# Two attention stages re-staged: queries and keys split in two, stacked to 48 rows a head through DRAM, and one unrolled pipeline over 128 heads

## The chip, the cores and the metric

The kernel runs on one core of one Trainium2 chip. The metric is the device time of one execution in microseconds (us). The kernel before took 2926.12 us, the median of three runs (2922.68 to 2927.64).

## The reference

Four transformer layers work one after the other on 8 sequences of 256 tokens, 256 channels, in float32. Each layer is an attention and a feed-forward part, each adding to x. Layers 0 and 3 have the same kind of attention, and only that is touched here:

```python
xn = layernorm(x)                       # (8, 256, 256)
q = xn @ Wq.T + bq;  k = xn @ Wk.T + bk;  v = xn @ Wv.T + bv
# 16 heads of 16 channels
scores = q_h @ k_h.T * 0.25             # causal, (256, 256) for each of 8 x 16 heads
x += concat(softmax(scores) @ v_h) @ Wo.T + bo
```

The other stages (two mixtures of experts before and after, the mixed attention of layer 1, the linear attention of layer 2, the dense feed-forward parts) stay as they are.

## The kernel before

Both stages are calls of `attention_small`, `a0` for layer 0 and `a3` for layer 3. The engines run their own instruction lists and meet at semaphores. The input xT lies in SBUF transposed: channels on partitions, tokens along the row. A batch is one of the 8 sequences. A loop (`Fori`) runs over seven batches and the eighth follows it; the 16 heads of a batch are written out.

For each batch, TensorE (`project`) multiplies the batch's 256 tokens, which GpSimd copied into `xb`, by the weights of keys, queries and values, into four PSUM tiles `ring0` to `ring3`. The bias of the values, and later that of the output, is one more matmul with a single row. A head has only 16 channels. So that a plain 128-row contraction gives the scores of one head, the keys are written 16 times into `kT`, each time multiplied by a column of `heads` that is 1 on that head's 16 channels and 0 elsewhere: ScalarE writes heads 0 to 7 (L1337) and VectorE heads 8 to 15 (L1376). Queries are used whole.

A head then passes through this chain. TensorE makes the scores, causal, in two matmuls (L1267: 128 queries by 128 keys; L1268: 128 by 256). VectorE scales and masks them from PSUM to `s` (L1388) and takes the negated maximum of each of the two row blocks (L1392). ScalarE takes the exponential and its row sums (L1349, with its accumulator reads). VectorE inverts the sums (L1398). GpSimd multiplies by the inverse (L1222), and after every second head sends one indirect DMA (L211) which carries token rows to the mixture of experts. TensorE turns the result in three transposes (`turn`, L1276). ScalarE copies even heads (L1359) and VectorE odd heads (L1404) to `pT`. TensorE multiplies by the values (`values`, L1288 and L1290) into `pv`; the value tile `v` is spaced so that each head's output lands on its own 16 partitions.

Within a batch the scores run four heads ahead of the turning (`AHEAD`). At a batch's end they do not run ahead: TensorE finishes the 16 heads, projects the next batch, waits for the copies, makes the first four scores, and then the output projection of the batch that ended (L1320, bias L1322), which VectorE adds to x (L1419).

SP issues the weight loads at a stage's start, in `a0` followed by the 10 MB of expert weights for the next stage (L1213, tile `wres`, 128 partitions of 16 x 1216 floats). No other plain DMA runs in these stages.

Of the kernel before, what the change touches and what calls it, by code (L numbers as in the profile page):

```python
# [9 lines left out]
ALU = mybir.AluOpType  # L10
# [7 lines left out]
P = 128  # L18
# [1117 lines left out]
AHEAD = 4  # L1136
SUMS_AHEAD = 3
SLOTS = 2 * AHEAD
# [3 lines left out]
def attention_small(nc, name, const, xT, w, scale, send, resident=()):  # L1142

    with ExitStack() as ctx:
        sp = Space(nc, ctx, name)  # L1150
        wts = {n: sp.sb(n, [P, KD, D]) for n in ("wq", "wk", "wv", "wo")}
        bq = sp.sb("bq", [P, KD])
        bk = sp.sb("bk", [P, KD])
        bv = sp.sb("bv", [1, D])
        bo = sp.sb("bo", [1, D])
        heads = sp.sb("heads", [P, HC])
        bkh = sp.sb("bkh", [P, HS])
        xb = sp.sb("xb", [P, KD, SEQ])
        qT = sp.sb("qT", [P, KD, SEQ])
        kT = sp.sb("kT", [P, HS, SEQ])  # L1160
        v = sp.sb("v", [P, QT * KD, HC * VS])
        s = sp.sb("s", [P, SLOTS, SC])
        nmax = sp.sb("nmax", [P, SLOTS, QT])
        rsum = sp.sb("rsum", [P, HS, QT])
        rinv = sp.sb("rinv", [P, HS, QT])
        pT = [sp.sb(f"pT{i}", [P, SC]) for i in range(2)]
        oT = sp.sb("oT", [P, KD, SEQ])
        ring = [sp.ps(f"ring{i}", [P, 512]) for i in range(4)]
        pv = sp.ps("pv", [P, KD, SEQ])
        ppT = [sp.ps(f"ppT{i}", [P, 512]) for i in range(2)]  # L1170
        pend = sp.ps("pend", [P, 512])
        w_in = sp.sem("w_in")
        bkh_ready = sp.sem("bkh_ready")
        xb_ready = sp.sem("xb_ready")
        q_done = sp.sem("q_done")
        k_done = sp.sem("k_done")
        v_done = sp.sem("v_done")
        q_ready = sp.sem("q_ready")
        k0_ready = sp.sem("k0_ready")
        k1_ready = sp.sem("k1_ready")  # L1180
# [4 lines left out]
        exp_ready = sp.sem("exp_ready")  # L1185
        turned = sp.sem("turned")
# [3 lines left out]
        inv_ready = sp.sem("inv_ready")  # L1190
        o_ready = sp.sem("o_ready")
        scaled = sp.sem("scaled")
        v_zeroed = sp.sem("v_zeroed")
        out_done = sp.sem("out_done")
        added = sp.sem("added")
        ident, ones, cmask = const["ident"], const["ones"], const["cmask"]
        spans = ((0, P), (P, SC))

        def batches(eng, run):

            with eng.Fori(0, NB - 1) as b:
                run(b, True)
            run(NB - 1, False)

        with nc.Block() as block:
            @block.sync
            def _(sync):
                for n in ("wq", "wk", "wv", "wo"):
                    sync.dma_start(wts[n][:, :, :], w[n]).then_inc(w_in, 16)
                for to, n in ((bq, "bq"), (bk, "bk"), (bv, "bv"), (bo, "bo"), (heads, "heads")):  # L1210
                    sync.dma_start(to[:, :], w[n]).then_inc(w_in, 16)
                for to, of, loaded in resident:
                    sync.dma_start(to, of).then_inc(loaded, 16)  # L1213

            @block.gpsimd
            def _(pool):
                def scale_rows(b, h):

                    pool.wait_ge(inv_ready, b * HS + (h + 1))
                    for t, (lo, hi) in enumerate(spans):  # L1220
                        rows = s[:, h % SLOTS, lo:hi]
                        last = nc.gpsimd.tensor_tensor(rows, rows, rinv[:, h, t:t + 1].broadcast_to([P, hi - lo]),  # L1222
                                                       ALU.mult)
                    last.then_inc(scaled, 1)

                def run(b, more):
                    for h in range(HS):
                        scale_rows(b, h)
                        if h % 2:
                            send(b * (HS // 2) + h // 2)  # L1230
                        if more and h == HC:

                            pool.wait_ge(v_done, b + 1)
                            nc.gpsimd.tensor_copy(xb[:, :, :], xT[:, :, bass.ds(b * SEQ + SEQ, SEQ)]
                                                  ).then_inc(xb_ready, 1)

                nc.gpsimd.tensor_copy(xb[:, :, :], xT[:, :, 0:SEQ]).then_inc(xb_ready, 1)
                for b in range(NB):
                    run(b, b + 1 < NB)

            @block.tensor
            def _(pe):
                def project(b):

                    pe.wait_ge(xb_ready, b + 1)
                    for n, bank, done in (("wk", 1, k_done), ("wq", 0, q_done)):
                        for c in range(KD):
                            to = ring[bank + c] if n == "wk" else ring[bank]
                            at = 0 if n == "wk" else c * SEQ
                            for k in range(KD):  # L1250
                                last = nc.tensor.matmul(to[:, at:at + SEQ], wts[n][:, k, c * P:(c + 1) * P], xb[:, k, :],  # L1251
                                                        start=(k == 0), stop=(k == KD - 1))
                        last.then_inc(done, 1)
                    for t in range(QT):
                        for k in range(KD):
                            nc.tensor.matmul(ring[3][:, t * D:(t + 1) * D], xb[:, k, t * P:(t + 1) * P],
                                             wts["wv"][:, k, :], start=(k == 0), stop=False)
# [1081 lines left out]
```

## Time and profile before

| | |
|---|---|
| median of 3 runs | 2926.12 us |
| the profiled execution | 2925.24 us |
| its span, first to last instruction | 2923.5 us |
| mean granted TensorE clock | 0.894 |
| busy, share of the span: PE, DVE, ACT, POOL | 79%, 54%, 45%, 32% |
| stage a0, by the timeline | 94.5 to 432.8 us |
| stage a3, by the timeline | 2393.6 to 2734.9 us |

The shares are averages over some twenty stages with different limits; the two stages at issue make up 680 of the 2924 us. PE is TensorE's matmul, PEld its weight load, DVE VectorE, ACT ScalarE, POOL GpSimd, SPq the queue that issues DMAs. A float32 matmul appears as two records.

### The profile page before, as it was taken

The page shows a single profiled execution, that of the slowest core. Times are in us where ns is not written, and L with a number is a line of the kernel's source. Part 1 is how long each engine was busy: PE and PEld are TensorE (multiplying, and loading weights), DVE is VectorE, ACT ScalarE, POOL GpSimd, SP SyncE. Part 2 cuts the span into 40 slices and gives each one's busy share as a digit, 9 for nine tenths or more (in the row PEclk, how much of TensorE's full clock was granted, in tenths as well). Part 3 has the DMA queues.
Part 4 walks back from the last instruction along what each step waited for, and adds up shares of the span by engine and source line. Part 5 has one row for each costly group of instructions (what it writes and reads, how often), then busy time and mean ns, then how long its engine had stood idle before and what let it go on. Part 6 is the DMA issues. An engine that isn't in the chain of part 4 may idle for free. (4 is left out here: it accounts for less than half of the span.)

```text
span 2923.5 us, 40558 instructions
## 1 busy us (share of the span) xinstructions
PE 2296.0 (79%) x11552; PEld 1807.6 (62%) x11552; DVE 1591.0 (54%) x4140; ACT 1322.2 (45%) x4166; POOL 927.1 (32%) x1053
## 2 busy tenths in 40 slices
PE   3599989997469999999998973468991229999787
PEld 2477776665247777777787762456880217777666
DVE  3677762224346666776684235553334577766324
ACT  1355553331157666666674121464770105555321
POOL 0355550005233333333340000540007006555325
PEclk9999999997689999999999985788995559999788
DMA  5400012323300000000000100611543000000354
GB/s 211 164 25 25 25 38 89 93 89 116 123 0 1 1 1 1 1 1 1 1 1 28 48 25 2 252 54 45 161 147 103 16 15 23 5 1 1 122 164 140
DMA packets 95446, 172.41 MB, mean 59 GB/s; under 512 B 17875, under 2 KB 73135, under 8 KB 93625
## 3 DMA queue, kind: packets, MB, share of 16 engines
q1 hardware_dynamic: 76856, 126.47, 12.7%
q0 software_dynamic: 18432, 44.05, 4.8%
q8 instruction: 74, 1.21, 0.2%
q14 instruction: 84, 0.68, 0.1%
HBM read 111.76 MB, written 65.01 MB: 60 GB/s over the span
## 5 line engine op out<-in xcount | busy, mean ns | idle before, releaser
L1222 POOL TENSOR_TENSOR a_s<-a_s,a_rinv 128x128 f32<-128x128 f32 (+1 forms) x512 | 243.3, 505 | 263.5 <-DVE a_rinv L1398 259.5
L1349 ACT ACTIVATE a_s<-a_s,a_nmax 128x128 f32<-128x128 f32 (+1 forms) x512 | 227.7, 446 | 181.5 <-DVE a_nmax L1392 177.2
L851 POOL DMA_INDIRECT f_yg<-y,l_slot x128 | 126.3, 987 | 383.8 <-issue 366.6
L1789 POOL TENSOR_TENSOR a_rcos<-a_qk,a_cos 128x1280 f32<-128x1280 f32 x32 | 93.2, 2911 | 403.8 <-ACT a_qk L1963 403.8
L211 POOL DMA_INDIRECT xg<-all_xn,l_slot_d x192 | 194.0, 1011 | 39.3 <-issue 39.3
L605 DVE TENSOR_TENSOR e_hid<-e_gate,e_pG 128x128 f32<-128x128 f32 (+1 forms) x192 | 59.3, 309 | 234.5 <-ACT e_gate L580 234.5
L1288 PE MATMUL a_pv<-a_pT,a_v 128*128 128x256 f32 x512 | 161.1, 397 | 17.8 <-ACT a_pT L1359 17.8
L2063 DVE SCALAR_TENSOR_TENSOR a_s<-a_pS,all_cmask 128x384 f32<-128x384 f32 x128 | 71.4, 558 | 172.9 <-PE a_pS L1870 172.9
L1268 PE MATMUL a_ring<-a_kT,a_qT 128*128 128x256 f32 x512 | 163.4, 403 | 0.0
L1392 DVE TENSOR_REDUCE a_nmax<-a_s 128x1 f32<-128x128 f32 (+1 forms) x512 | 156.7, 348 | 8.8
L1388 DVE SCALAR_TENSOR_TENSOR a_s<-a_ring,all_cmask 128x384 f32<-128x384 f32 x256 | 139.9, 547 | 25.0 <-PE a_ring L1268 22.5
L183 PE MATMUL n_pT<-all_ident,all_xn 128*128 128x128 f32 x128 | 33.9, 411 | 145.8 <-DVE all_xn L173 141.9
L494 POOL DMA_INDIRECT e_yg<-y,l_slot x64 | 61.0, 953 | 266.7 <-SPq L468 246.9
L1337 ACT ACTIVATE a_kT<-a_ring,a_bkh,a_heads 128x256 f32<-128x256 f32 x128 | 60.1, 575 | 181.7 <-PE a_ring L1251 181.7
L890 ACT ACTIVATE f_gate<-f_pg 128x512 f32<-128x512 f32 x60 | 35.9, 599 | 223.9 <-PE f_pg L770 223.9
L1276 PE MATMUL a_ppT<-all_ident,a_s 128*128 128x128 f32 x768 | 128.0, 276 | 8.0 <-POOL a_s L1222 8.0
L1896 PE MATMUL a_pout<-a_wo,a_oT 128*128 128x256 f32 x512 | 131.9, 380 | 2.4 <-ACT a_oT L2002 1.4
L1831 PE MATMUL a_pq<-a_wq,all_xT 128*128 128x512 f32 x256 | 123.8, 607 | 9.8 <-ACT a_qk L1963 9.8
L952 DVE TENSOR_TENSOR f_hid<-f_gate,f_pu 128x512 f32<-128x512 f32 x60 | 41.3, 688 | 157.0 <-PE f_pu L770 119.2
L1972 ACT ACTIVATE a_e<-a_qk,a_top 128x128 f32<-128x128 f32 x320 | 123.5, 390 | 1.5 <-DVE a_top L2039 1.5
L1799 POOL TENSOR_TENSOR a_src<-a_rcos,a_rsin 128x1280 f32<-128x1280 f32 x32 | 94.2, 2944 | 84.7 <-PE a_pt L1859 84.4
L528 PE MATMUL e_pG<-l_wres,e_xgT 128*128 (+1 forms) x448 | 119.0, 388 | 1.8 <-ACT e_xgT L573 1.8
(289 smaller groups left out, 6481.5 us busy)
## 6 DMA issues: line engine op xcount, KB each, us to landing
e_xs<-xg SPq DMA_DIRECT2D x176, 128.0 KB, 2.2
y<-e_ys SPq DMA_DIRECT2D x176, 128.0 KB, 1.7
l_wres<-in_L_resident SPq DMA_DIRECT2D x3, 4224.0 KB
xg<-blank_zeros SPq DMA_DIRECT2D x4, 3072.0 KB
s_w<-in_L_bank SPq DMA_DIRECT2D x32, 384.0 KB, 4.0
l0e_wres<-in_L_resident SPq DMA_DIRECT2D x4, 2432.0 KB
f_w<-in_L_bank SPq DMA_DIRECT2D x16, 448.0 KB, 3.2
f_w<-in_L_shared SPq DMA_DIRECT2D x14, 448.0 KB, 3.7
```

The lines of the kernel that those rows point to most:

```text
L211: nc.gpsimd.indirect_dma_start(out=xg[:, :], out_offset=bass.IndirectOffsetOnAxis(ap=slot_d[:, t, j:j + 1], axis=0), in_=xn[:, t, :], in_o ...
L851: nc.gpsimd.indirect_dma_start(out=yg[i % GR][:, :], out_offset=None, in_=y, in_offset=bass.IndirectOffsetOnAxis(ap=slot[:, t, j:j + 1], a ...
L1222: last = nc.gpsimd.tensor_tensor(rows, rows, rinv[:, h, t:t + 1].broadcast_to([P, hi - lo]), ALU.mult)
L1268: nc.tensor.matmul(ring[h % 4][:, P:SC], qT[:, c, P:SEQ], kT[:, h, :], start=True, stop=True).then_inc(s_done, 1)
L1276: last = nc.tensor.transpose(ppT[h % 2][:, i * P:(i + 1) * P], s[:, h % SLOTS, i * P:(i + 1) * P], ident[:, :])
L1288: nc.tensor.matmul(pv[:, c, :], v[:, c, j * P:(j + 1) * P], pT[h % 2][:, 0:SEQ], start=first, stop=final, skip_group_check=True)
L1349: last = nc.scalar.activation(s[:, h % SLOTS, lo:hi], s[:, h % SLOTS, lo:hi], ACT.Exp, bias=nmax[:, h % SLOTS, t:t + 1], accum_out=rsum[:, ...
L1388: nc.vector.scalar_tensor_tensor(out=s[:, h % SLOTS, :], in0=ring[h % 4][:, 0:SC], scalar=scale, in1=cmask[:, :], op0=ALU.mult, op1=ALU.ad ...
L1392: last = nc.vector.tensor_reduce(nmax[:, h % SLOTS, t:t + 1], s[:, h % SLOTS, lo:hi], AX_X, ALU.max, negate=True)
L1831: last = nc.tensor.matmul(pq[:, :], tokens(b, k, t), wq[:, k, gr, :], start=(k == 0), stop=(k == KD - 1))
L1896: last = nc.tensor.matmul(pout[:, t, :], oT[H % 2][:, t * P:(t + 1) * P], wo[:, n % HKV * GQ + h, :], start=(h == 0 and t == 0), stop=(h = ...
L1972: last = nc.scalar.activation(e[:, t, h, :], qk[:, t, h, :], ACT.Exp, bias=top[:, at:at + 1], accum_out=total[:, at:at + 1])
```

## The change

`attention_small` is rewritten. The parts:

- **Projection in pieces.** Queries and keys are projected in pieces of 128 output channels by 512 tokens (two batches, a chunk): four pieces a chunk, 16 a stage, into one PSUM tile `pj`. ScalarE writes the biased piece rounded to fp32r (`hi`), VectorE the rest (`lo` = exact minus `hi`).
- **Through DRAM.** SP stores both parts to `qk_rows`, and loads them back stacked: for each head 48 rows, queries (hi, lo, hi), keys (hi, hi, lo), so that one fp32r contraction over 48 rows gives hi*hi + lo*hi + hi*lo. Even heads lie at partitions 0 to 47, odd ones at 64 to 111. A load of half a batch (8 heads) is 12 DMAs of 64 KB, 64 runs of 1 KB each; 24 a batch, and four stores of 256 KB a batch.
- **Scores** are two fp32r matmuls from those tiles, in a ring of two PSUM tiles in place of four.
- **One list of slots.** The batch loop goes; 128 heads a stage run in one unrolled sequence. In slot n, TensorE makes scores n+4, turns n and applies values n-1; ScalarE takes exponentials n+3 and then rounds the slot's piece (`round_piece`); VectorE inverts n+2, masks and takes maxima n+4, and then makes `lo` (`rest_piece`). Slots run from -24 to 131. The pieces of a chunk are put 24 slots ahead, every third slot; a batch's values are projected in two halves, 6 slots ahead; its output two slots after its last head.
- **Biases.** The bias of the values is added by VectorE as it copies them; that of the output is added to x once, by GpSimd, at the stage's start. The single-row matmuls, `xb` and its copies, `heads`, `bkh` and the 16 masked key copies go.
- **Copies.** `pv` and `oT` are double, and `oT` is copied by ScalarE. The expert weights of `a0` are issued behind the first two loads, not at once.

```diff
-        kT = sp.sb("kT", [P, HS, SEQ])
+        stack = [[sp.sb(f"{n}s{i}", [P, HC // 2, SEQ], F32R) for i in range(2)] for n in "qk"]
-        ring = [sp.ps(f"ring{i}", [P, 512]) for i in range(4)]
+        ring = [sp.ps(f"ring{i}", [P, 512]) for i in range(2)]
...
+        def piece_at(slot):
+            c, left = divmod(slot + LEAD, 2 * HS)
+            return 4 * c + left // 3 if left % 3 == 0 and left < 12 and 0 <= c < NC else None
...
+                def store(i):
+                    c, n, k = PIECES[i]
+                    for part, ready, tiles, out in ((0, hi_ready, hi, hi_out), (1, lo_ready, lo, lo_out)):
+                        sync.wait_ge(ready, i + 1)
+                        sync.dma_start(qk_rows[n, part, k * P:(k + 1) * P, c * CHUNK:(c + 1) * CHUNK],
+                                       tiles[i % 2][:, :].bitcast(F32)).then_inc(out[i % 2], 16)
+                def load(b, half):
+                    c = b // 2
+                    for i in range(2):
+                        sync.wait_ge(hi_out[i], 16 * 2 * (c + 1))
+                        sync.wait_ge(lo_out[i], 16 * 2 * (c + 1))
+                    after(sync, s_done, HS * b + HC * (half - 1))
+                    for n, parts in ((0, (0, 1, 0)), (1, (0, 0, 1))):
+                        for odd in range(2):
+                            for j, part in enumerate(parts):
...
+                                sync.dma_start(stack[n][half][at:at + DH, :, :].bitcast(F32), rows).then_inc(stacked[half], 16)
+                for i in range(4):
+                    store(i)
+                for c in range(NC):
+                    load(2 * c, 0)
+                    load(2 * c, 1)
+                    if c == 0:
+                        for to, of, loaded in resident:
+                            sync.dma_start(to, of).then_inc(loaded, 16)
+                    load(2 * c + 1, 0)
+                    if c + 1 < NC:
+                        for i in range(4 * c + 4, 4 * c + 8):
+                            store(i)
+                    load(2 * c + 1, 1)
...
+                def piece(i):
+                    c, n, k_out = PIECES[i]
+                    after(pe, hi_ready, i)
+                    after(pe, lo_ready, i)
...
+                    for k in range(KD):
+                        last = nc.tensor.matmul(pj[:, :], wts[("wq", "wk")[n]][:, k, k_out * P:(k_out + 1) * P],
+                                                xT[:, k, c * CHUNK:(c + 1) * CHUNK], start=(k == 0), stop=(k == KD - 1))
+                    last.then_inc(piece_done, 1)
...
+                def scores(H):
+                    b, h = divmod(H, HS)
+                    half, a, r = h // HC, h % HC // 2, 64 * (h % 2)
+                    if h % HC == 0:
+                        pe.wait_ge(stacked[half], 16 * 12 * (b + 1))
+                    after(pe, s_read, H - 1)
+                    q, k = (stack[n][half][r:r + ST, a, :] for n in range(2))
+                    nc.tensor.matmul(ring[H % 2][:, 0:P], q[:, 0:P], k[:, 0:P], start=True, stop=True)
+                    nc.tensor.matmul(ring[H % 2][:, P:SC], q[:, P:SEQ], k[:, :], start=True, stop=True).then_inc(s_done, 1)
...
+                for slot in SLOTS_ALL:
+                    if 0 <= slot + 4 < NH:
+                        scores(slot + 4)
+                    i = piece_at(slot)
+                    if i is not None:
+                        piece(i)
+                    if 0 <= slot < NH:
+                        turn(slot)
...
+                    if 0 <= slot - 1 < NH:
+                        values(slot - 1)
...
+                def round_piece(i):
+                    n, k = PIECES[i][1:]
+                    act.wait_ge(piece_done, i + 1)
+                    after(act, hi_out[i % 2], 16 * (i // 2))
+                    after(act, lo_ready, i - 1)
+                    nc.scalar.activation(hi[i % 2][:, :], pj[:, :], ACT.Identity,
+                                         bias=bias[n][:, k:k + 1]).then_inc(hi_ready, 1)
...
+                def rest_piece(i):
+                    dve.wait_ge(hi_ready, i + 1)
+                    after(dve, lo_out[i % 2], 16 * (i // 2))
+                    nc.vector.scalar_tensor_tensor(out=lo[i % 2][:, :], in0=pj[:, :], scalar=bias[n][:, k:k + 1],
+                                                   in1=hi[i % 2][:, :], op0=ALU.add, op1=ALU.subtract).then_inc(lo_ready, 1)
```

## Rows read from the trace of the kernel before

**Rows 1.** Windows: length, busy us of PE, PEld, DVE, ACT, POOL, then granted clock, DMA share, GB/s

```profile
95.00:114.00 19.00, 9.85 (x28) 7.03 (x28) 8.66 (x12) 4.49 (x10) 0.17 (x1) 1.00 0.96 373
194.00:234.00 40.00, 37.78 (x218) 31.06 (x217) 28.84 (x84) 23.07 (x84) 23.79 (x41) 1.00 0.07 26
2480.00:2520.00 40.00, 39.02 (x216) 32.42 (x216) 28.63 (x82) 21.94 (x79) 22.84 (x40) 0.96 0.02 6
1800.00:1950.00 150.00, 74.40 (x343) 62.25 (x344) 89.22 (x169) 69.63 (x142) 69.21 (x72) 0.76 0.38 149
```

**Rows 2.** Timeline of PE, one head in mid-batch (start, length, idle before)

```profile
167.10 0.39 PE L1267 MATMUL a_ring<-a_kT,a_qT 128*128 128x128 f32 x2
167.32 0.60 PE L1268 MATMUL a_ring<-a_kT,a_qT 128*128 128x256 f32 x2
167.75 0.49 PE L1276 MATMUL a_ppT<-all_ident,a_s 128*128 128x128 f32 x3
168.08 0.60 PE L1288 MATMUL a_pv<-a_pT,a_v 128*128 128x256 f32 x2
...
168.74 0.39 PE L1267 MATMUL a_ring<-a_kT,a_qT 128*128 128x128 f32 x2
```

**Rows 3.** Timeline of PE between two batches

```profile
188.43 1.89 PE L1251 MATMUL a_ring<-a_xb,a_wk 128*128 128x256 f32 x8
...
191.89 1.03 PE L1256 MATMUL a_ring<-a_wv,a_xb 128*128 128x256 f32 x4
...
196.10 0.46 PE L1267 MATMUL a_ring<-a_kT,a_qT 128*128 128x128 f32 x2 [0.88 <-DVE a_v L1380]
...
198.79 1.03 PE L1320 MATMUL a_pend<-a_wo,a_oT 128*128 128x256 f32 x4
...
202.06 0.49 PE L1267 MATMUL a_ring<-a_kT,a_qT 128*128 128x128 f32 x2
```

**Rows 4.** Timeline of POOL: first and last work of both stages, one boundary

```profile
119.78 1.89 POOL L1222 TENSOR_TENSOR a_s<-a_s,a_rinv 128x128 f32<-128x128 f32 x4 [24.61 <-DVE a_rinv L1398]
...
201.80 1.89 POOL L1222 TENSOR_TENSOR a_s<-a_s,a_rinv 128x128 f32<-128x128 f32 x4 [14.53 <-DVE a_rinv L1398]
...
204.90 1.89 POOL L1222 TENSOR_TENSOR a_s<-a_s,a_rinv 128x128 f32<-128x128 f32 x4
...
424.98 1.01 POOL L211 DMA_INDIRECT xg<-all_xn,l_slot_d  x1 [0.16 <-issue]
...
2414.98 1.89 POOL L1222 TENSOR_TENSOR a_s<-a_s,a_rinv 128x128 f32<-128x128 f32 x4 [20.72 <-DVE a_rinv L1398]
...
2727.10 1.01 POOL L211 DMA_INDIRECT xg<-all_xn,l_slot_d  x1 [0.16 <-issue]
```

**Rows 5.** Timeline of DVE, start and end of two heads' work

```profile
171.56 0.56 DVE L1404 COPY a_pT<-a_ppT 128x384 f32<-128x384 f32 x1 [0.37 <-PE a_ppT L1276]
...
174.32 0.15 DVE L1398 RECIPROCAL a_rinv<-a_rsum 128x2 f32<-128x2 f32 x1
```

**Rows 6.** One line's instructions: duration ns min/median/max, first and last start

```profile
L907 DVE TENSOR_TENSOR f_wl<-f_w,f_wh x30: 683/684/726, 676.1 to 2896.7; 128x512 fp32r<-128x512 f32 x30
```

**Rows 7.** Timeline of PE, the first projections of both stages

```profile
103.35 3.78 PE L1251 MATMUL a_ring<-a_xb,a_wk 128*128 128x256 f32 x8 [26.25 <-DMA a_heads<-in_heads]
...
2399.95 3.55 PE L1251 MATMUL a_ring<-a_xb,a_wk 128*128 128x256 f32 x8 [39.98 <-DMA a_heads<-in_heads]
```

**Rows 8.** Timeline of PE, fp32r matmuls of another stage

```profile
684.25 0.39 PE L770 MATMUL f_pu<-f_xh,f_wl 128*128 128x512 f32 x1
684.48 0.39 PE L770 MATMUL f_pu<-f_xh,f_wh 128*128 128x512 f32 x1
```

**Rows 9.** Timeline of SPq, an issue behind big transfers and one in an idle queue

```profile
35.40 1.25 SPq L271 DMA_DIRECT2D r_order<-in_order  x1
...
95.39 0.42 SPq L1209 DMA_DIRECT2D a_wv<-in_L_wv  x1
```

**Rows 10.** DMA issues: KB each, median us from issue to landing

```profile
e_xs<-xg SPq DMA_DIRECT2D x176, 128.0 KB, 2.2
y<-e_ys SPq DMA_DIRECT2D x176, 128.0 KB, 1.7
```

More of the change, by code:

```diff
@@ L1151, in attention_small @@
         wts = {n: sp.sb(n, [P, KD, D]) for n in ("wq", "wk", "wv", "wo")}
[L1152 to L1159, printed above, removed]
-        kT = sp.sb("kT", [P, HS, SEQ])
+        bias = [sp.sb(f"bias{i}", [P, KD]) for i in range(2)]
+        bvb = sp.sb("bvb", [P, D])
@@ L1189, in attention_small, with after, batch_at @@
         pv_done = sp.sem("pv_done")
-        inv_ready = sp.sem("inv_ready")
         o_ready = sp.sem("o_ready")
-        scaled = sp.sem("scaled")
-        v_zeroed = sp.sem("v_zeroed")
         out_done = sp.sem("out_done")
         added = sp.sem("added")
[L1196 to L1203, printed above, removed]
+        ident = const["ident"]
+        spans = ((0, 0, P), (1, P, SC))
+        PIECES = [(c, n, k) for c in range(NC) for n in range(2) for k in range(KD)]
+        def after(eng, sem, value):
+            if value > 0:
+                eng.wait_ge(sem, value)
+        def piece_at(slot):
+            c, left = divmod(slot + LEAD, 2 * HS)
+            return 4 * c + left // 3 if left % 3 == 0 and left < 12 and 0 <= c < NC else None
+        def batch_at(slot, ahead):
+            b, left = divmod(slot + ahead, HS)
+            return b if left == 0 and 0 <= b < NB else None
+        SLOTS_ALL = range(-LEAD, NH + 4)
         with nc.Block() as block:
@@ L1223, in scale_rows @@
+                for H in range(NH):
+                    pool.wait_ge(inv_ready, H + 1)
+                    for t, lo_, hi_ in spans:
+                        rows = s[:, H % RING, lo_:hi_]
+                        last = nc.gpsimd.tensor_tensor(rows, rows, rinv[:, H % RING, t:t + 1].broadcast_to([P, hi_ - lo_]),
                                                        ALU.mult)
                     last.then_inc(scaled, 1)
[L1226 to L1235, printed above, removed]
@@ L1237, in _ @@
-                nc.gpsimd.tensor_copy(xb[:, :, :], xT[:, :, 0:SEQ]).then_inc(xb_ready, 1)
-                for b in range(NB):
-                    run(b, b + 1 < NB)
+                    if H % 2:
+                        send(H // 2)
             @block.tensor
             def _(pe):
[L1243 to L1253, printed above, removed]
+                sent = {"pieces": 0, "values": 0}
```

318 lines of the change are left out of this document (148 added, 170 removed).

## The prediction

> **What bounds the kernel now.** The table of windows comes first. In both stages PE is busy 38 to 39 of every 40 us, DVE 29, ACT 23, POOL 24 [rows 1]. A busy PE may be waiting in the array, so the next view is PE's timeline in mid-batch: one head takes 1.64 us (167.10 to 168.74) without a gap, of which scores 0.65, turning 0.33, values 0.65 or 0.66 [rows 2]. POOL's timeline shows the same from the other side: two heads in 3.10 us back to back (201.80 to 204.90), that is 1.55 a head, and then 14.53 us of nothing at the boundary of two batches [rows 4]. PE's timeline there says what fills the hole: projection from 188.43 to the wait that ends at 196.10, four heads' scores until 198.79, output projection until 202.06 [rows 3]. So the stage is PE, head by head, plus a boundary at which the pipe empties. A batch takes 39.87 us in a0 by the starts of POOL's bursts. POOL works from 119.78 to 426.0 in a0 (306.2 us) and from 2414.98 to 2728.1 in a3 (313.1 us) [rows 4].
>
> **PE's work for a batch after the change.** Turning 16 x 0.33 = 5.3 and values 16 x 0.65 = 10.4 stay [rows 2]. The pieces cost what the projection of q and k costs now: 188.43 to 191.89, 3.46 us a batch, since the product is the same size [rows 3]. Values are four 256-column float32 matmuls' worth, half of 3.46, 1.73; output the same 1.73, in place of 198.79 to 202.06 = 3.27, because the bias matmuls go [rows 3]. Scores: no row has an fp32r matmul as narrow as 128 or 256 columns or with 48 rows. The nearest are fp32r with 512 columns, started every 0.23 us [rows 8], against four times that for float32 (a 256-column one takes 0.43 [rows 2]). In proportion 384 columns would take 0.17. The weight loads set a floor: the transposes, 128 columns each, follow each other at 0.11 [rows 2], and two score matmuls have two weight loads, 0.22. The upper end is no gain at all, 0.65. I take 0.22, nearest the fp32r rows, so 3.5 a batch. Sum 5.3 + 10.4 + 3.5 + 3.5 + 1.7 + 1.7 = 26.1 us (33.0 at the upper end).
>
> **DVE.** Two heads occupy it from 171.56 to 174.47, 2.91 us, so 23.3 for 16 [rows 5]. It loses eight masked key copies and the copy of oT. It gains two `lo` pieces of 512 elements (0.68 each by the row of the same form [rows 6], 0.72 with the step to the next), two value copies of 256 elements, which I put at 0.42 each (between 0.29 and 0.68 in proportion), and keeps the add to x at about 0.7. Sum 23.3 + 1.4 + 0.8 + 0.7 = 26.3. **POOL**: 8 x 3.10 = 24.8 [rows 4]; the copy of xb goes, the bias add of 4096 elements lies at the start, under the prologue below. **ACT**: 23.0 now [rows 1], less ten key and query copies of 0.46 (4.6), plus two `hi` pieces and one oT copy of about 0.6: 20.3.
>
> So PE 26.1, DVE 26.3 and POOL 24.8 stand side by side, and the pace is a little over the largest, because they wait for each other. The place is a piece slot. There PE has scores 0.22, a piece 1.73, turning and values, 2.9 us; ScalarE can round only after the piece, and VectorE, in order, stands at `lo` behind it: piece 1.73 + 0.6 + semaphores = 2.4 us after the scores, while its own masking and maxima take 1.1. Some 1.2 us are lost unless PE is ahead of DVE, and two score tiles let it be ahead by about one head. Three slots with one piece cost DVE 3 x 1.46 + 0.7 + 0.3 left over = 5.4; 12 of 32 slots are of that kind: 21.6 us. The other 20 go at POOL's 1.55 or DVE's 29.1 + 3.2 of values and adds, plus waits for the value projections: 34. That is 55.6 for two batches, **28 us a batch**. From below it is 26.3 (DVE alone). 8 x 28 = 224 in place of 306.2 and 313.1: **-171 us**.
>
> **The prologue.** Now it is from the end of the weight wait (103.35, 2399.95) to POOL's first work, 16.4 and 15.0 us [rows 4, 7]. After: four pieces in series, since `pj` is one tile. PE ran its first eight records of 256 columns in 3.5 to 3.8 us [rows 7] where it takes 1.73 later [rows 3]: it had stood idle for 26 and 40 us, and runs at the lower of its two levels (1.2 and 2.4 GHz) at first. A piece is the same work: 3.4 cold or 1.7 warm, then hi 0.6, lo 0.7, semaphores 0.2. One or two cold, the rest warm: 16.5 (13 to 20). Then the last stores, issue 0.9 and landing near 2 (128 KB out took 1.7 [rows 10]): 3. Then 12 loads issued at 0.47 (0.42 and the step [rows 9]), 5.6, and landing 2.2 [rows 10]: 7.8. Then the chain of the first head, 5.7 as now. Together 33, so +16.6 in a0, less 2 because the expert weights no longer compete with the weights (the window before carries 373 GB/s [rows 1]), and +18 in a3: **+33**. The drain loses two bias matmuls on its path: **-2**.
>
> **The new wait: SP's order.** A chunk's first three quarters are loaded well ahead. But load (2c+1, second half) is queued behind the four stores of the next chunk. Their last piece is in slot 32c+17, and the load is needed by scores 32c+24 in slot 32c+20. From `lo` ready: two stores 0.9, 12 loads 5.6, landing 2.2, 8.7 us; cover is the rest of slot 17 and slots 18 and 19, 3.8. PE then stands in scores with turning and values behind it, POOL runs dry two heads later. About 5 us, three times a stage: **+30** for both. If stores and loads land as they issue it is 3 each, if they queue 7. In a0 the first load of batch 1 is also behind the expert weights: 10 MB at 373 GB/s [rows 1] is 26.7 us, started about 3.4 after the first scores; needed about 26 after them. Landing near 33: **+7** (0 if the queue interleaves).
>
> **Sum**: 2925.2 - 171 + 33 - 2 + 30 + 7 = 2822 us. The profiled execution, 2925.24, is 0.9 below the median, which is nothing here. About 0.2% (6 us) is what a measurement can tell from no change.
>
> **A rule weighed.** PE's clock was granted in full in a0 and 0.96 in a3 with PE 95% busy or more, 0.76 in a stretch where it was busy half the time [rows 1]. The new pipe has PE at 26.1 of 28, with more and shorter waits. The Trainium skill (TensorE: Matmul & The Clock Gate, Part 1) says that the array runs at half rate by default, that activity releases it and idleness brings it back. By that rule the prologue, with PE idle for some 11 us between pieces and scores, starts the pipe at 1.2 GHz; the rows of both first projections agree. The same page (Why this matters for your kernels, the row on small-K matmuls) says that a 32-row matmul takes as long as a 128-row one and gains only where row groups run together; then the 48 rows themselves save nothing and the gain is the single fp32r pass. By the first rule with every piece of both prologues at 1.2 GHz, an estimate, the time would be 2832; by the rows, which let one or two pieces be slow, it is 2822, and the sum goes by these.
>
> **Rivals.**
> - *Little is lost between the engines.* For it: PE leads by one head, and POOL has slack in piece slots. Pace 26.5, the SP waits at 3: 2822 - 24 - 12 = 2786, and 2760 with no SP waits. Against: three engines within 6%, each in order, rarely meet their own sum. Chance 0.22, times 2760 to 2795.
> - *PE is dearer.* Narrow fp32r matmuls gain less, or the clock slips. If the 128-column one stays at its present 0.22 and the other at 0.11, PE is 27.9, pace 29.5: +24, 2846 (still within my forecast). With no gain in scores PE is 33, pace 34: 2918. With a mean clock of 0.87: 30 + 1.5 = 31.5 a batch, 2878. Chance 0.20 for 2860 to 2918.
> - *The clock stays low and the kernel is slower.* This decides at the pace that eats the gain: 28 + 103/16 = 34.4 us a batch. PE's 26.1/c + 1.5 reaches it at a granted clock of 0.79. At the 0.76 of the window of another stage [rows 1] it is 35.8: +125, 2947. For it: shorter bursts, a PE that waits in piece slots. Against: what PE has to do fills 93% of the pace even at 2.4 GHz, and a slower clock makes it busier. Chance 0.05.
> - *SP's issue bounds.* 28 DMAs a batch at 0.47 are 13 us. In a busy queue one issue took 1.25 [rows 9]; then they are 35 us a batch, and the prologues grow by 19: 2822 + 112 - 30 + 19 = 2923, no change. Against: 2 MB a batch is 75 GB/s, a fifth of what the window of 373 GB/s carried. Chance 0.03, half of it on the slow side.
>
> **Numbers.** Forecast 0.50, times 2795 to 2860. Faster by over 0.2%: 0.50 + 0.22 + 0.20 + half of what stays, 0.92; within 0.2%: 0.02; slower 0.06. The range takes the forecast, two thirds of the low rival and half of the dear one: 2770 to 2885.
>
> **What would show it.** Masked key copies and single-row matmuls gone; PE's scores near 0.22 a head; POOL's idle at batch boundaries gone and its pace 1.7 to 1.8 a head; first POOL work 33 us after the weights; three waits of PE on stacked loads of some 5 us a stage, in slots 32c+20, and one of some 7 early in a0; ACT about 20 us a batch. Wrong if PE's clock falls under 0.9, if DVE waits for `hi` over 1 us at each piece, or if loads take over 1 us to issue.

## The result and the profile after

| | before | after |
|---|---|---|
| median | 2924.40 us (4 runs) | 2889.32 us (4 runs, 2883.79 to 2896.41) |
| ratio | | 0.9886 (95%: 0.9854 to 0.9918) |
| span of the profiled execution, clock | 2923.5 us, 0.894 | 2881.9 us, 0.882 |
| stage a0, first a_wq issue to first load of the next stage | 339.1 us | 325.3 us |
| stage a3 | 343.4 us | 319.4 us |

The change makes the kernel 1.1% faster. The forecast was 2822 us with a range from 2770 to 2885, so the time lies 4 us above the range and 67 above the forecast.

POOL's timeline, first and last work of both stages, answers to [rows 4]:

```profile
131.19 0.97 POOL L1267 TENSOR_TENSOR a_s<-a_s,a_rinv 128x128 f32<-128x128 f32 x2 [20.65 <-DVE a_rinv L1430]
...
412.57 1.01 POOL L211 DMA_INDIRECT xg<-all_xn,l_slot_d  x1 [0.16 <-issue]
...
2419.15 0.97 POOL L1267 TENSOR_TENSOR a_s<-a_s,a_rinv 128x128 f32<-128x128 f32 x2 [22.52 <-DVE a_rinv L1430]
...
2692.04 1.01 POOL L211 DMA_INDIRECT xg<-all_xn,l_slot_d  x1 [0.16 <-issue]
```

From first to last work, called the pipe below, it is 282.4 us in a0 (306.2 before) and 273.9 in a3 (313.1). The prologues, from a stage's start to that first work, grew by 11.4 us in a0 (131.19 against 119.78) and by 16.7 in a3 (38.1 against 21.4). Over both stages the pipes give -63, the prologues +28 and the ends -3, together -38 of the 41.6 us by which the spans differ.

PE's timeline, one plain head in mid-batch, answers to [rows 2]:

```profile
281.44 0.60 PE L1325 MATMUL a_pv<-a_pT,a_v 128*128 128x256 f32 x2
281.87 0.38 PE L1327 MATMUL a_pv<-a_pT,a_v 128*128 128x128 f32 x2
282.19 0.32 PE L1306 MATMUL a_ring<-a_ks,a_qs 48*128 48x128 f32 x1
282.35 0.33 PE L1307 MATMUL a_ring<-a_ks,a_qs 48*128 48x256 f32 x1
282.61 0.55 PE L1313 MATMUL a_ppT<-all_ident,a_s 128*128 128x128 f32 x3
283.00 0.60 PE L1325 MATMUL a_pv<-a_pT,a_v 128*128 128x256 f32 x2
```

The starts tell what each part costs. Scores, 282.19 to 282.61, are 0.42 us (0.65 before, 0.22 forecast). But turning became 0.39 (0.33), and from the second values matmul to the next scores it is 0.32 where it was 0.22. A head is 1.56 us, not the forecast's 1.20, and was 1.64. PE has no gap in it. The weight loads at the same place:

```profile
281.87 0.19 PEld L1327 LDWEIGHTS a_pv<-a_pT,a_v 128*128 128x128 f32 x1
282.18 0.18 PEld L1306 LDWEIGHTS a_ring<-a_ks,a_qs 48*128 48x128 f32 x1
...
282.61 0.31 PEld L1313 LDWEIGHTS a_ppT<-all_ident,a_s 128*128 128x128 f32 x3
```

The load for the scores starts at 282.18 and its matmul at 282.19; that of the turning at 282.61 together with its matmul. On both edges of the 48-row pair nothing is loaded ahead of its matmul by more than 0.01 us.

PE's timeline at its waits for stacked loads, with SP's below:

```profile
127.86 0.48 PE L1306 MATMUL a_ring<-a_ks,a_qs 48*128 48x128 f32 x2 [8.60 <-DMA a_ks<-qk_rows]
...
164.72 0.47 PE L1306 MATMUL a_ring<-a_ks,a_qs 48*128 48x128 f32 x1 [5.59 <-DMA a_ks<-qk_rows]
...
191.56 0.47 PE L1306 MATMUL a_ring<-a_ks,a_qs 48*128 48x128 f32 x1 [3.67 <-DMA a_ks<-qk_rows]
...
265.10 0.47 PE L1306 MATMUL a_ring<-a_ks,a_qs 48*128 48x128 f32 x1 [4.35 <-DMA a_ks<-qk_rows]
```

```profile
254.79 0.32 SPq L1227 DMA_DIRECT2D qk_rows<-a_hi  x1
255.57 0.39 SPq L1227 DMA_DIRECT2D qk_rows<-a_lo  x1
256.13 4.38 SPq L1242 DMA_DIRECT2D a_qs<-qk_rows  x6
260.55 2.78 SPq L1242 DMA_DIRECT2D a_ks<-qk_rows  x6
```

The last store leaves at 255.57, the twelve loads behind it are issued until 263.3, and PE resumes at 265.10. The first of the four waits is the prologue's. A fifth wait in a0 is 2.84; a3 has 2.94, 4.19 and 3.98 beside its prologue. Without the prologues that is 16.5 and 11.1 us. What a wait leaves behind is in the windows (columns as in [rows 1]):

```profile
160.00:164.00 4.00, 0.00 (x0) 0.00 (x0) 0.19 (x2) 0.00 (x0) 0.96 (x2) 1.00 1.08 337
164.00:168.00 4.00, 3.28 (x11) 2.65 (x11) 1.24 (x4) 1.40 (x5) 0.97 (x2) 0.52 0.25 95
168.00:172.00 4.00, 4.00 (x12) 2.76 (x12) 2.44 (x7) 0.98 (x4) 1.97 (x3) 0.50 0.09 33
172.00:176.00 4.00, 4.00 (x13) 2.10 (x11) 0.97 (x3) 1.26 (x4) 0.00 (x0) 0.70 0.00 0
...
204.00:208.00 4.00, 4.00 (x27) 3.40 (x28) 3.40 (x12) 3.06 (x12) 3.05 (x6) 1.00 0.09 33
...
226.00:262.00 36.00, 34.58 (x177) 25.25 (x175) 26.62 (x79) 21.49 (x77) 23.46 (x40) 1.00 0.34 116
262.00:297.00 35.00, 31.90 (x176) 26.22 (x177) 24.40 (x76) 19.50 (x74) 23.59 (x40) 0.90 0.32 92
```

PE stood idle from 159.1 to 164.7. Then the granted clock is 0.50, its lower level of 1.2 GHz, for some 9 us, although PE is busy 4.00 of 4 us: 12 or 13 records in a window where 27 run at the full clock. Behind the other waits it is 5 to 10 us in a0 and 5 to 13 in a3, some 63 us behind all seven. The first heads of each pipe also run at 0.50, in a0 from 127.9 to 140. The clock over both pipes is 0.92 and 0.93.

The new pieces of work in a0 (groups by line, mean ns after the comma):

```profile
L1406 DVE SCALAR_TENSOR_TENSOR a_lo<-a_pj,a_bias,a_hi 128x512 fp32r<-128x512 f32 x16 | 12.0, 751 | 34.0 <-ACT a_hi L1367 34.0
L1367 ACT ACTIVATE a_hi<-a_pj,a_bias 128x512 fp32r<-128x512 f32 x16 | 11.0, 689 | 74.2 <-PE a_pj L1284 74.2
L1413 DVE TENSOR_TENSOR a_v<-a_pj,a_bvb 128x256 f32<-128x256 f32 x16 | 6.8, 423 | 3.5 <-PE a_pj L1295 2.6
```

In the order of these lines, the forecast had 680, 600 and 420 ns.

### The profile page after: what moved, and what is told of

The parts are those of the page before. It is cut to its first block and busy times, and to the rows that moved or that the text cites. A ratio compares the mean times of both kernels' runs of the same rounds, so it can differ in the third digit from the quotient of the medians.

```text
span 2881.9 us, 38632 instructions
## 1 busy us (share of the span) xinstructions
PE 2228.6 (77%) x10912; PEld 1715.8 (60%) x10912; DVE 1539.7 (53%) x4040; ACT 1285.0 (45%) x4054; POOL 942.1 (33%) x1039
## 5 line engine op out<-in xcount | busy, mean ns | idle before, releaser
L1313 PE MATMUL a_ppT<-all_ident,a_s 128*128 128x128 f32 x768 | 148.6, 306 | 0.0
L1306 PE MATMUL a_ring<-a_ks,a_qs 48*128 48x128 f32 x256 | 87.5, 345 | 47.9 <-DMA a_ks<-qk_rows 45.1
L2105 DVE SCALAR_TENSOR_TENSOR a_s<-a_s,a_rinv,a_g 128x128 f32<-128x128 f32 (+1 forms) x256 | 117.4, 500 | 4.5
```

Source lines behind the costliest of these rows:

```text
L1313: last = nc.tensor.transpose(ppT[H % 2][:, i * P:(i + 1) * P], s[:, H % RING, i * P:(i + 1) * P], ident[:, :])
```

## The experiments

Four theories are tested: *rows* (scores on 48 rows keep weights from being loaded ahead, so a head costs 0.35 us more), *clock* (PE pays for each wait a second time at half clock), *queue order* (a wait comes from what stands ahead of the loads on SP), and the rival *GpSimd or VectorE sets the pace*. Kernels that ran once are compared by the spans of their profiled executions: 2881.9 us is that of the changed kernel. The spans of its four runs go from 2881.9 to 2894.5, so a few us between two kernels mean nothing. Diffs are against the changed kernel unless said; lines left out are marked by three dots.

| kernel | median (runs) | span | clock |
|---|---|---|---|
| earlier pieces | 2857.21 (4), ratio 0.9773 (0.9750 to 0.9797) | 2861.5 | 0.886 |
| float32 scores | 3066.68 (1) | 3064.8 | 0.856 |
| scores twice | 3000.46 (1) | 2998.6 | 0.862 |
| half of GpSimd's work | 2881.40 (1) | 2879.5 | 0.883 |
| 128 rows | 2837.61 (4), ratio 0.970 (0.966 to 0.974) | 2837.9 | 0.882 |
| 128 rows, twice | 2852.59 (1) | 2850.8 | 0.879 |
| 128 rows, float32 | 2888.52 (1) | 2886.7 | 0.889 |
| earlier pieces, experts' weights later | 2864.61 (4), ratio 0.980 (0.976 to 0.984) | 2862.9 | 0.886 |
| the three together | 2827.21 (6), ratio 0.9663 (0.9632 to 0.9694) | 2827.4 | 0.886 |
| 128 rows, earlier pieces, weights spread | 2804.17 (5), ratio 0.9587 (0.9569 to 0.9605) | 2803.8 | 0.891 |
| the same with filler | 2806.71 (5), ratio 0.9600 (0.9581 to 0.9619) | 2803.8 | 0.893 |
| the same (no filler), half of GpSimd's work | 2803.31 (1) | 2801.5 | 0.890 |

**Earlier pieces.** The pieces of a chunk start 30 slots ahead.

```diff
-    LEAD = 24
+    LEAD = 30
```

> The four pieces of the next chunk are put 30 slots ahead in place of 24, so that their stores leave SP's queue before slot 32c+12 and the last quarter's loads are issued in time. Theory W (SP's order makes PE wait, and each wait is followed by a stretch at the lower clock): the three later waits of PE on the stacked loads in each stage go (some 11 us in a0, 11 in a3), and the windows of 35 us with a granted clock of 0.86 to 0.90 go to 1.00, worth another 10 to 13 us a stage; the span falls by 40 to 50 us, to about 2835. Rival (the low clock comes from the pieces and value projections, not from the waits): only the waits go, 20 to 25 us, and the clock stays at 0.86 in every second window.

All seven waits on stacked loads behind the prologues go (27.6 us), and the clock is 1.00 in both stages from the end of batch 0 on. The pipes shrink to 266.0 and 258.1 us, by 32.2; in the medians the kernel gains 32 too, in the spans 20. In a0 5.2 us of another wait appears, at 162 to 167: PE waits for ScalarE's copy to `pT`, and ScalarE stood 7.12 us before it rounded a piece. By the code it waits there until an earlier store has landed, and the stores share the queue with the 10 MB. Queue order was the cause of the seven waits. The expectation of 40 to 50 us was missed: the stretches at half clock gave back little beyond the waits, 4.6 us in the pipes, or 9.8 with the new wait set aside, where 20 to 26 were expected.

**Float32 scores, 48 rows.** The same tiles, read as float32.

```diff
-                    q, k = (stack[n][half][r:r + ST, a, :] for n in range(2))
+                    q, k = (stack[n][half][r:r + ST, a, :].bitcast(F32) for n in range(2))
```

> The same stacked tiles of 48 rows are read as float32, so each score matmul is two records and TensorE never changes between float32 and fp32r. Theory S (a change of type between neighbouring matmuls costs about 0.1 us, since the next weights are not loaded ahead): a plain head takes 0.65 + 0.33 + 0.65 = 1.63 us against 1.56, the turning goes back from 0.39 to 0.33 and the last values from 0.31 to 0.22. Rival R (48 rows, or the change of row groups, costs it): the gaps stay and the head takes 1.8 us or more, the span grows by over 60 us. Rival G (GpSimd paces the head at 1.55): 1.63 as well, but POOL then shows idle time in plain slots.

The gaps stay: last values to scores 0.32, turning 0.38. So they do not come from a change of type between neighbours. A head at full clock is 1.98, 0.42 more, which is 108 us over 256 heads; the span grew by 183. The windows below show long stretches at the lower clock, which is where the rest is to be looked for; it was not measured by itself.

**Scores twice, 48 rows.** Both score matmuls are issued two times.

```diff
-                    nc.tensor.matmul(ring[H % 2][:, 0:P], ...)
-                    nc.tensor.matmul(ring[H % 2][:, P:SC], ...).then_inc(s_done, 1)
+                    for again in range(2):
+                        nc.tensor.matmul(ring[H % 2][:, 0:P], ...)
+                        last = nc.tensor.matmul(ring[H % 2][:, P:SC], ...)
+                    last.then_inc(s_done, 1)
```

> Both score matmuls of every head are issued twice into the same place. Theory S and any theory by which PE paces the head: each head grows by the bare price of 128 and 256 columns in fp32r, 0.17 to 0.22 us, 45 to 60 us over both stages; if the second pair costs 0.42 as the first seems to, there is no cost of the change of type and fp32r is itself dear at this width. Rival G (GpSimd paces): no change of a plain head's 1.56 us.

A head takes 1.78 us (values start at 284.00 and again at 285.78), so the second pair costs 0.22 us: the forecast's price for a pair is right between its own kind. What was missed stands at the pair's edges. 0.22 over 256 heads is 56 us, the span grew by 117; here too the clock is at its lower level for longer (windows below).

**Half of GpSimd's work.** GpSimd scales only the first row block; the second stays unscaled.

```diff
-                    for t, lo_, hi_ in spans:
+                    for t, lo_, hi_ in spans[0:1]:
```

> GpSimd scales only the first row block of every head and leaves the second (256 columns) unscaled, so its two heads take about 1.9 us in place of 3.1. Theory S (PE paces): a plain head stays at 1.55 to 1.56 us and the span within 10 us of 2882. Rival G (GpSimd paces): a plain head falls towards PE's or DVE's 1.46 or less and the span by 20 us or more.

The span falls by 2.4 us, and a plain head (one without a piece or a value projection in its slot) takes 1.56 us as before (280.60 to 282.15): GpSimd does not set the pace.

**128 rows.** `s` is a ring of 7 to make room. Each head's query rows lie in their own column block of a tile that is zero elsewhere, and the contraction runs over all partitions; the other head's keys meet zeros. GpSimd zeroes the tiles once at the stage's start.

```diff
-        stack = [[sp.sb(f"{n}s{i}", [P, HC // 2, SEQ], F32R) for i in range(2)] for n in "qk"]
+        stack = [[sp.sb(f"{n}s{i}", [P, w_, SEQ], F32R) for i in range(2)] for n, w_ in (("q", HC), ("k", HC // 2))]
...
-                    q, k = (stack[n][half][r:r + ST, a, :] for n in range(2))
+                    q, k = stack[0][half][:, h % HC, :], stack[1][half][:, a, :]
```

> Scores contract over all 128 rows: the query tile holds each head with zeros on every row but its own 48, the key tile is shared by two heads, and both are zeroed once; the ring of s is 7 in place of 8 so that it fits. fp32r stays. Theory R (a matmul on 48 of 128 rows costs PE about 0.3 us a head, because the weights on either side of it are not loaded ahead): the last values go back from 0.31 to 0.22, scores from 0.42 to about 0.28, turning from 0.39 to 0.33, so PE can do a head in 1.25 us, GpSimd's 1.55 paces plain heads and PE catches up after pieces; span 40 to 60 us less than 2882. Theory S (the change between float32 and fp32r costs it): a plain head stays at 1.56. Theory C (with 48 rows the clock stays at its lower level although PE is busy throughout): after each wait on a load the stretch at 0.50 is 4 to 6 us in place of 10 to 11.

PE's timeline, then its weight loads:

```profile
272.37 0.38 PE L1335 MATMUL a_pv<-a_pT,a_v 128*128 128x128 f32 x2
272.51 0.31 PE L1314 MATMUL a_ring<-a_ks,a_qs 128*128 128x128 f32 x1
272.65 0.34 PE L1315 MATMUL a_ring<-a_ks,a_qs 128*128 128x256 f32 x1
272.82 0.49 PE L1321 MATMUL a_ppT<-all_ident,a_s 128*128 128x128 f32 x3
273.15 0.60 PE L1333 MATMUL a_pv<-a_pT,a_v 128*128 128x256 f32 x2
```

```profile
284.59 0.19 PEld L1314 LDWEIGHTS a_ring<-a_ks,a_qs 128*128 128x128 f32 x1
...
284.83 0.35 PEld L1321 LDWEIGHTS a_ppT<-all_ident,a_s 128*128 128x128 f32 x3
```

The matmuls to these loads start at 284.62 and 284.93: the loads are 0.03 and 0.10 us ahead. Values to scores is 0.14, scores 0.31, turning 0.33, a head of PE's own work 0.44 + 0.14 + 0.31 + 0.33 = 1.22. Set against 0.33 for turning and 0.65 for values, the pair costs 0.24 net, close to the 0.22 of the forecast. That is 0.34 us a head less than on 48 rows, 87 us over 256 heads. The pipes shrink by 51 us and the spans differ by 44, although the waits are no shorter (20.0 and 11.1): every second plain head waits 0.21 us for VectorE's copy to `pT`, and two take 2.92 us, so VectorE now holds the pace at 1.46. The Trainium skill (TensorE: Matmul & The Clock Gate, Step-by-step: what each phase is for) says that the engine pulls a weight load ahead of running matmuls when the row groups don't conflict or the load goes to the background buffer; the trace agrees that 128-row loads go ahead, and shows that those beside 48-row matmuls don't.

**128 rows, twice; 128 rows, float32.** The doubling and the float32 reading as above, on 128 rows.

> As e5_rows128, with the two score matmuls issued twice. With 48 rows this put the clock at 0.50 to 0.74 in windows in which PE was busy 36 of 36 us, and the span at 2999. Theory C: on 128 rows the clock is 1.00 in steady state, a head takes 0.22 us more than in e5_rows128, partly hidden behind GpSimd, and the span is under 2890. Rival (it is fp32r or the amount of work that holds the clock down): the clock is again between 0.5 and 0.75, the span near 3000.

> 128 contraction rows, but the scores in float32 instead of fp32r: the fourth corner of rows (48, 128) and type (fp32r, float32). Theory that the narrow rows cause both the gaps and the low clock: score instructions near 0.33 and 0.65 us, the values' second half at 0.14 to 0.2 and turning at 0.33, a head near 1.6 to 1.7 us, granted clock at or near 1.00 in the windows behind 190 us, span 2885 to 2925. Rival (the low clock with float32 or doubled scores on 48 rows came from the amount of TensorE work and not from the rows): clock 0.5 to 0.7 in 190 to 262 us and a span over 3000.

The square of spans: fp32r 2881.9 on 48 rows and 2837.9 on 128, float32 3064.8 and 2886.7. The square of PE's plain heads at the full clock: fp32r 1.56 and 1.22, float32 1.98 and 1.64. The 48 rows cost 0.34 us a head in either type. Windows of the two float32 kernels, 48 rows, then 128:

```profile
190.00:226.00 36.00, 36.00 (x112) 26.38 (x112) 14.53 (x45) 10.92 (x41) 13.73 (x23) 0.50 0.19 56
226.00:262.00 36.00, 36.00 (x141) 26.23 (x141) 17.33 (x52) 13.77 (x51) 15.65 (x27) 0.70 0.13 41
```

```profile
190.00:226.00 36.00, 36.00 (x231) 32.42 (x230) 27.96 (x87) 22.08 (x83) 25.80 (x44) 0.96 0.28 87
226.00:262.00 36.00, 32.47 (x186) 25.99 (x185) 23.43 (x68) 19.06 (x67) 21.22 (x37) 0.99 0.34 118
```

PE is busy 36.00 of 36 us in both first windows. With 48 rows the clock stays at 0.50 all that time, with 128 it is 0.96. It fell in both at 189.9, some 0.9 us behind the end of a wait for loads (1.87 us long on 48 rows, 2.55 on 128), and was back at 247.6 with 48 rows and at 193.1 with 128. Doubled scores show the same: 0.54 and 0.74 in these windows on 48 rows (span +117), 1.00 and 0.95 on 128 (+13). So a PE that was busy without a break did not have its clock back here; with the same matmuls on 128 rows it did. The amount of work as the cause is refuted. Where the clock is up, 48-row scores do not lower it: the float32 kernel on 48 rows holds 1.00 from 250 to 286.

**Expert weights later.** Earlier pieces, and the 10 MB issued behind both loads of batch 1; then the same with 128 rows ("the three together" in the table).

```diff
                     load(2 * c, 1)
-                    if c == 0:
-                        for to, of, loaded in resident:
-                            sync.dma_start(to, of).then_inc(loaded, 16)
...
                     load(2 * c + 1, 1)
+                    if c == 0:
+                        for to, of, loaded in resident:
+                            sync.dma_start(to, of).then_inc(loaded, 16)
```

> e1_lead30 with the expert weights of a0 issued behind the loads of the second batch, 48 rows as in the change. In e1_lead30 PE stood at 160 to 167 us behind stores that shared the queue with the 10 MB. Theory W: that wait and the low clock behind it go, 8 to 12 us less than e1_lead30 (2857), to about 2847. Rival (the transfers hold up others wherever they are put): no change, or a wait of the expert stage for its weights.

> e5_rows128, with the pieces 30 slots ahead and the expert weights of a0 issued behind the loads of the second batch. If theories W, R and C hold together: no wait on stacked loads after the first, clock 1.00 after the first 15 us of the pipe, pace near 27 to 28 us a batch, span 2790 to 2815. If GpSimd and the piece slots leave more, 2830.

The early wait goes and a longer one comes: 11.8 us at 207.3 on 48 rows, and on 128 rows (PE's timeline):

```profile
206.92 0.48 PE L1314 MATMUL a_ring<-a_ks,a_qs 128*128 128x128 f32 x1 [14.35 <-DMA a_ks<-qk_rows]
```

These are the loads of batch 2, now the ones behind the 10 MB. On 48 rows the median is 7 us above that of earlier pieces alone (2864.61 against 2857.21, from two chips; the spans are 2862.9 and 2861.5), so at best nothing is gained: what a later place gives back, a later wait takes. Both expectations (some 2847, and 2790 to 2815 for the three together) were missed by this wait.

**Weights spread.** The 10 MB are four transfers of 2.5 MB (the expectation below speaks of two). They go apart, one behind each of the four chunks' last load, with 128 rows and earlier pieces.

```diff
                     load(2 * c, 1)
-                    if c == 0:
-                        for to, of, loaded in resident:
-                            sync.dma_start(to, of).then_inc(loaded, 16)
...
                     load(2 * c + 1, 1)
+                    for to, of, loaded in resident[c:c + 1]:
+                        sync.dma_start(to, of).then_inc(loaded, 16)
```

> 128-row scores and LEAD 30, with the two large resident transfers each issued behind the stacked loads of a later batch instead of both behind those of the second. Theory of queue order: the 14 us wait of TensorE at about 207 us of the first attention stage goes, because it was for stacked loads that lay behind both transfers; span near 2815, 8 to 15 below the kernel that issues both together. Rival (the bytes have to be moved some time in this stage, and any place makes a wait of the same size): a wait of about 14 us stands elsewhere, span stays at 2827 within 4.

PE waits for stacked loads in the prologue alone, and the span is 23.6 us below that of the three together. This is the best kernel, with a median of 2804.17. Both pipes are 237.3 us, and in a0 from the addition to x of the first batch to that of the last (178.4 to 373.8) the clock is 1.00. In plain heads VectorE is now the one without gaps (its timeline):

```profile
190.02 0.61 DVE L1432 TENSOR_REDUCE a_nmax<-a_s 128x1 f32<-128x128 f32 x2
190.55 0.55 DVE L1441 COPY a_pT<-a_ppT 128x384 f32<-128x384 f32 x1
...
192.94 0.61 DVE L1432 TENSOR_REDUCE a_nmax<-a_s 128x1 f32<-128x128 f32 x2
193.47 0.55 DVE L1441 COPY a_pT<-a_ppT 128x384 f32<-128x384 f32 x1
```

Two heads take 2.92 us.

**Weights spread, half of GpSimd's work.** Again GpSimd scales only the first row block (the diff is that of "Half of GpSimd's work", made to the kernel with weights spread).

> The kernel with spread resident transfers, but GpSimd multiplies only the first row block of each head by the inverse sums, the second stays unscaled: some 0.5 to 1.3 us less GpSimd work a head. Theory that after the repair of the score rows GpSimd sets the pace of a plain head (1.55 us in its timeline, TensorE waiting 0.2 a head for the chain behind it): plain heads fall to VectorE's 1.45 or so, some 80 plain heads a stage by 0.1 us or a little more, 10 to 20 us less over both stages, span 2784 to 2794. Rival (TensorE still sets it, as it did on 48 rows, where the same edit gave 2.4 us): within 4 us of 2803.8.

The span falls by 2.3 us: the expectation that GpSimd now sets the pace failed. PE's idle time in plain heads is the same with and without GpSimd's half, 0.21 or 0.22 us in every second head, and it is for VectorE's copy to `pT`. So VectorE sets the pace of plain heads, at 1.46; this is read from the timelines, and no run made VectorE's work less.

**Filler in the prologue's wait.** Nine matmuls on 128 rows, whose result nobody reads, ahead of the first scores of the kernel with weights spread.

```diff
+                    if H == 0:
+                        for i in range(9):
+                            nc.tensor.matmul(ppT[0][:, :], wts["wq"][:, 0, 0:P], xT[:, 0, 0:CHUNK], start=True, stop=True)
```

> The kernel with spread resident transfers, and nine matmuls whose result nobody reads, on 128 rows, put in front of the first scores while these wait for the stacked loads. Theory that the clock falls to 0.50 because TensorE idles in that wait and stays there some 10 us after it: with the filler the first windows behind the wait show a clock near 1.00, and the span falls by 5 to 10 us (5 us or so of time at half clock in each of two stages). Rival (the idle of the prologue is not what sets the clock, or the other engines pace these first heads): clock in those windows as before, span within 3 us of the kernel without filler or a little above it.

Windows without, then with filler:

```profile
124.00:128.00 4.00, 0.00 (x0) 0.00 (x0) 0.00 (x0) 0.00 (x0) 0.00 (x0) 0.51 0.45 139
128.00:132.00 4.00, 2.03 (x7) 1.45 (x7) 1.67 (x5) 0.50 (x3) 0.00 (x0) 0.50 0.47 140
...
136.00:140.00 4.00, 3.59 (x9) 2.38 (x10) 2.98 (x10) 2.22 (x9) 3.77 (x8) 0.50 0.11 41
```

```profile
124.00:128.00 4.00, 4.00 (x11) 1.71 (x9) 0.00 (x0) 0.00 (x0) 0.00 (x0) 1.00 0.46 142
128.00:132.00 4.00, 2.08 (x10) 1.12 (x8) 1.97 (x6) 0.80 (x4) 0.00 (x0) 1.00 0.52 137
...
136.00:140.00 4.00, 3.90 (x9) 2.69 (x10) 2.67 (x8) 1.91 (x9) 3.81 (x7) 0.50 0.18 66
```

With the filler the clock stays at 1.00 until 134. Then it goes to 0.50 all the same, behind the pipe's first heads, in which PE waits for VectorE between scores and is busy 2.1 of 4 us; both kernels are back at 1.00 at 142. Both spans are 2803.8. The idle wait does lower the clock behind it, but these first heads hang on VectorE's chain, so nothing is won.

## Why the prediction was wrong, point by point

**What held.** What bounded the kernel before held, and so did the direction and the end of the boundaries between batches. The new operations take 751, 689 and 423 ns against 680, 600 and 420. The prologues together are +28 against +33, with one cold piece (3.78 us) in a0 and two (3.78 and 3.47) in a3, where one or two were forecast; the ends are -3 against -2. SP's order made three waits a stage in the slots named, 2.84 to 4.35 us (22 in all) against 5 each (30), and 5.59 against 7 for batch 1. The first experiment shows that the order makes them. The pipe did start at 0.50, as the rule weighed in the prediction had it.

**The step that failed** is "I take 0.22, nearest the fp32r rows, so 3.5 a batch. Sum ... 26.1 us", and with it the pace of 28 us a batch. The pair costs 0.22 only beside its own kind. With 128-row matmuls on its edges it costs a head 0.36 more: 1.56 in place of 1.20. Of this, 0.34 goes away when the scores use 128 rows. Priced from rows of the earlier pieces' trace, PE in one pipe is 128 x 1.56 + 12 pieces x 1.8 + 15 halves of values x 0.9 + 8 outputs x 1.73 = 248.6 us, 24.6 over the 224 that were forecast for the pipe. The prediction's bound of no gain in scores (33 a batch) did hold this, at 31, but the value was taken near the other bound.

The prediction looked at columns and type and put the rows in the contraction at nothing. Yet the kernel before has matmuls on a single row, those of the biases, and their price was in its trace (PE's timeline, inside the stretch of [rows 3]):

```profile
198.79 1.03 PE L1320 MATMUL a_pend<-a_wo,a_oT 128*128 128x256 f32 x4
199.75 0.69 PE L1322 MATMUL a_pend<-a_bo,all_ones 1*128 1x256 f32 x2
200.38 1.13 PE L1320 MATMUL a_pend<-a_wo,a_oT 128*128 128x256 f32 x4
201.44 0.69 PE L1322 MATMUL a_pend<-a_bo,all_ones 1*128 1x256 f32 x2
202.06 0.49 PE L1267 MATMUL a_ring<-a_kT,a_qT 128*128 128x128 f32 x2
```

The output projection takes 3.27 us and without its two bias matmuls was put at 1.73, so each of them costs 0.77, where 256 float32 columns on 128 rows take 0.43 [rows 2]. That is 0.34 more, at a granted clock of 1.00, and the weight loads on both sides (199.75 and 200.37) start with their matmuls. The prediction took these 1.54 us off the output and didn't ask why two single-row matmuls were so dear. The Trainium skill (TensorE: Matmul & The Clock Gate, Why this matters for your kernels) says that a single 32-row matmul takes as long as a 128-row one; the prediction read this as a cap on the gain, and the traces show a loss beside it.

**What was left out** is the clock behind each wait. The waits were priced at their own length. The pipes without their waits took 282.4 - 16.5 and 273.9 - 11.1, together 528.7, against 448 forecast: 80.7 too many. Of them 49 are the heads (2 x 24.6). The other 31 are a difference and in part open. Half of the 63 us at 0.50 behind the seven waits would be just this, but the kernel with earlier pieces has none of these stretches and its pipes gained only 4.6 us beyond the waits, or 9.8 with its new wait set aside. The other 22 or so stand in its pipes too, whose mean clock is 0.96 and 0.97: first heads at 0.50 (for 18 us in each stage, against 12 and 11 in the changed kernel), and slots in which PE waits for the others. No run parts these two; the filler gained nothing by lifting the clock in some of the first heads, which speaks for the second. The rival with a mean clock of 0.87 named the mechanism, too strong in size (0.92 and 0.93 came), and the range of the dear rival (2860 to 2918) is where the time fell. Its two parts, dearer scores and a clock that slips, shared a chance of 0.20.

**The balance:** 2822 + 81 (pipes) - 9 (waits 27.6 for 37) - 5 (prologues) - 1 (ends) = 2888, against 2883.8 of the profiled execution; the other stages were 4 us shorter.

**Slips in the sums.** None of them moves the forecast. Four pieces at 16.5 us have two cold ones in them already, so with all four cold in both prologues the rule weighed gives some 2829, not 2832. For a0 the rows of the granted clock did not show a slow start: the window from 95 to 114 has 1.00 [rows 1] while the first projection took 3.78 us, twice its later 1.89; in a3 the clock of the kernel before reads 0.50 up to 2403. By the sizes in the change, stores and loads are 2.6 MB a batch, not 2. The chances 0.50, 0.22 and 0.20 make 0.92 without the half of what stays. And one of the signs of being wrong came: VectorE waits for `hi` 1.34 to 1.44 us at nearly every piece of the pipes.

**GpSimd and VectorE.** The forecast set DVE (26.3), PE (26.1) and POOL (24.8) side by side. With the rows repaired and the waits gone the pipe takes 237 us against the 224 forecast, with VectorE back to back in plain heads: the model of the three engines was near, 6% short, once PE's price was right.

## What to carry to other kernels

A matmul on few rows must be priced with its neighbours: look whether its weight load, and the next one, start ahead of their matmuls, and look for any narrow matmul that the kernel already has, even one of a bias. Padding the contraction with zeros to all 128 rows gained 44 us here. A wait of TensorE costs its length and, behind it, a stretch at half clock; taking away 27.6 us of waits gained 32 in the pipes, so the second part was there but small. And a large transfer put in one piece in a queue made the next loads late in both places tried; split over four places with slack, it made none late.

## What the hardware showed that was not expected

- Beside 128-row matmuls, a pair of 48-row ones costs a head 0.34 us more than the same pair on 128 rows, in fp32r (1.56 against 1.22) and in float32 (1.98 against 1.64). A single-row matmul between 128-row ones costs 0.34 more than one on 128 rows (0.77 against 0.43). Beside its own kind a 48-row pair costs 0.22. What in the engine makes it, the number of rows or the change from one set of rows to another, no run parts.
- With PE busy 36.00 of 36 us on 48-row scores in float32 the granted clock stayed at 0.50; on 128 rows it was 0.96. With fp32r scores it was back 5 to 13 us after a wait on 48 rows (seven waits) and 5 to 6 us after it on 128 (six waits; behind a seventh, of 3.61 us, it did not fall). Why rows matter to the clock no run here tells.
- The rule weighed in the prediction, that activity releases the clock, does not foretell these windows by the profile's busy time: the engine was busy in all of them.
